# Means of the first two tiles by products over columns of the transposed input, later loads of the row-major input, and a re-ordered start, product stage and tail

## The chip, the cores and the metric

The kernel runs on one core of a Trainium2 chip. The metric is the device time of one execution in microseconds (us). Three executions of the kernel before took 243.49, 243.72 and 243.82 us, so the median is 243.72 us. The execution that was profiled took 243.56 us.

The core has five engines with instruction streams of their own: TensorE (PE in the profile; its weight loads are listed as PEld), VectorE (DVE), ScalarE (ACT), GpSimd (POOL) and SyncE (SP, which here only issues transfers). They wait for each other through semaphores. Transfers issued by SP, ACT and POOL share the core's 16 DMA engines.

## The reference, cut to what matters

The input x has 8 x 256 rows of 512 numbers, which the kernel sees as 16 tiles of 128 rows.

```python
xn = _layernorm(x, axis=-1)                         # (x - m) / sqrt(v + 1e-5)
q = (xn @ Wq.T + bq)                                # 32 heads of 128
q_sel = (elu(q) + 1)[:, :, ::4, :]                  # every fourth head: 8 heads, 1024 columns
num = einsum('bshd,hde->bshe', q_sel, M)
den = einsum('bshd,hd->bsh', q_sel, z)[..., None] + 1e-6
out_heads = repeat(num / den, 4, axis=2)
out = x + out_heads.reshape(b, s, 4096) @ Wo.T + (xn @ (w_int8 * w_scale) + b)
```

The keys and values do not reach the output. Since each retrieved head is repeated four times, the four matching blocks of Wo can be added first. Since M comes before Wo, each head needs one matrix P_g = M_g times that summed block (128 x 512).

## The kernel before, in words

**Precision.** Each of the large products is made of three passes in the format fp32r: the operands are split into a high part (`_hi`, a copy rounded by ACT) and a low part (`_lo`, the rest, subtracted by DVE), and PE computes hi times hi, hi times lo and lo times hi. Each pass is one instruction with 128 rows of weights and 512 columns.

**Stages.** For each tile t:

- the mean and the variance of the rows come from the row-major tile x (`moments`: one BN_STATS, one BN_AGGR, and the variance plus epsilon), and GpSimd makes the reciprocal root (`rstd_of`);
- the mean is spread over all partitions by a PE transpose (`spread_mean`) and subtracted from the transposed tile xT. For tiles 0 to 2 DVE does it straight from the accumulator bank (`center_first`, `center`); from tile 3 on ACT copies the mean (`copy_mean`) and POOL subtracts it (`center`);
- ACT makes `xT_hi` and DVE `xT_lo`; PE makes q in two halves (`product_q(t, 0)` and `(t, 1)`, 12 instructions each) and the dense part (`product_dense(t)`, 12 instructions into the one bank `dense_ps`, which DVE has to empty by `add_dense(t - 1)` first);
- DVE scales and biases q (`add_bias`), ACT takes the exponential (`exp_of`), DVE forms s = elu + 1 (`make_s`); POOL multiplies by z (`times_z`), DVE sums and inverts (`denominator`), ACT scales (`make_a`), DVE transposes 32 x 32 blocks (`turn_blocks`), and 16 small transfers move the blocks to where they belong (`spread_blocks`, issued by SP, at the end also by ACT and POOL as `spread_group` and `spread_last_group`). ACT and DVE split the result (`copy_aT_hi`, `split_aT_lo`), and PE makes `product_attn(t)` of 24 instructions. DVE adds it to x, and SP stores the tile.

**Start.** Wq (2 MB) comes in eight pieces or fewer, and PE works on tiles 0 and 1 together, in an order written out by hand, as the pieces arrive. Before that, PE runs products of zeros (`keep_busy`).

**Wo.** The four blocks of Wo arrive in two halves j: the first block by a plain load (`load_wo(j)`), three more by POOL transfers that add while they write (`add_wo(r, j)`, 1 MB each). Each of these waits until the one before it on the same half has landed, and everything behind it on POOL waits with it. When all three have landed on half 0, PE may make P_0 to P_3 (`product_P`, one plain fp32 product of 512 columns each); half 1 gives P_4 to P_7. The banks `attn_ps` alternate, so P_g for g >= 2 waits until DVE has split P_(g-2) (`split_P_lo`).

**Order.** There is no scheduler. Each engine's order is the order of the calls in its block (`@block.sync`, `gpsimd`, `scalar`, `vector`, `tensor`), written out by hand up to tile 6 and by a loop from tile 7 (`LEAD`) on. Within one engine nothing overtakes.

The whole of it is below, with the line numbers that the profile uses.

Of the kernel before, what the change touches and what calls it, by code (L numbers as in the profile page):

```python
# [18 lines left out]
def retrieval_and_dense(nc, x_d, xT_d, WqT_d, bq_d, WoT_d, MT_d, z_d, w_d, wscale_d, b_d, out_d):  # L19
# [19 lines left out]
    with ExitStack() as ctx:  # L39
# [28 lines left out]
        ident = sb("ident", [P, P])  # L68
        e_and_sz = sb("e_and_sz", [P, E + G * (D + 1)])
# [34 lines left out]
        wq_half_in = [sem(f"wq_half_in{i}") for i in range(4)]  # L104
        wq_in = [sem(f"wq_in{k}") for k in range(2, K)]
# [5 lines left out]
        consts_set = sem("consts_set")  # L111
        eps_set = sem("eps_set")
# [77 lines left out]
        def _(sp):  # L190
# [11 lines left out]
            def load_wq(k):  # L202
                sp.dma_start(WqT_raw[:, k, :], WqT_d[0, k]).then_inc(wq_in[k - 2], 16)

# [38 lines left out]
            load_wo(1)  # L243
            sp.dma_start(MT[:], MT_d).then_inc(M_in, 16)
            load_x(4)
            load_xT(4)
            sp.dma_start(z_b[:], z_d.unsqueeze(0).to_broadcast([P, E])).then_inc(z_in, 16)
            sp.dma_start(b_b[:], b_d.unsqueeze(0).to_broadcast([P, HID])).then_inc(b_in, 16)
            for t in range(5, FIRST_LENT):
                load_x(t)  # L250
                load_xT(t)
# [27 lines left out]
        def _(pool):  # L279
            def rstd_of(t):  # L280
                pool.wait_ge(vareps_ready, t + 1)
# [10 lines left out]
            def scale_w():  # L292
                pool.wait_ge(wscale_in, 16)
                pool.wait_ge(w_cast, 2)
                nc.gpsimd.tensor_tensor(wd_raw[:, K // 2:, :], w_f32[:, K // 2:, :], wd_raw[:, K // 2:, :], ALU.mult
# [27 lines left out]
            def spread_last_group(t):  # L323
                pool.wait_ge(a_turned, t + 1)
                pool.wait_ge(aT_lo_ready, 2 * t - 2)
                for j in range(4):
                    nc.gpsimd.dma_start(aT_place(t)[j * 32:(j + 1) * 32, 3, :],
                                        sbuf_s[96:128, t % SRING, j * E // 4:(j + 1) * E // 4]).then_inc(aT_in_by_pool[t - FIRST_SHARED - 1], 16)

            nc.gpsimd.memset(neg_half[:], -0.5).then_inc(consts_set, 1)  # L330
# [8 lines left out]
            pool.wait_ge(wd_by_pool, 1)  # L339
# [4 lines left out]
            add_wo(1, 1)  # L344
            rstd_of(4)
# [200 lines left out]
        def _(dve):  # L546
            def statistics(t):
                dve.wait_ge(x_in[t], 16)
                if t >= 2:
                    dve.wait_ge(meanvar_ready, t - 1)  # L550
# [455 lines left out]
```

## Time and profile before

| what | value |
|---|---|
| median of three executions | 243.72 us |
| profiled execution | 243.56 us |
| its span, first to last instruction | 241.7 us |
| PE busy | 234.1 us, 97% of the span |
| DVE busy | 178.0 us, 74% |
| ACT busy | 119.6 us, 49% |
| POOL busy | 108.4 us, 45% |
| moved by transfers | 34.83 MB |

Read it with three things in mind. The span leaves out 1.9 us of the execution that lie around it. PE's busy time counts overlapping records and the products of zeros at the start, so a busy PE says that it had an instruction in flight, not that it was at its peak. And a share is an average over the start, the stage in which Wo is added, the steady loop and the tail, which have different limits.

### The profile page before, as it was taken

To read this page: it belongs to the slowest core of one execution; us is meant where nothing else is said; L and a number is where in the kernel's file an instruction comes from. 1 tells how busy PE (TensorE), PEld (TensorE's weight loads), DVE (VectorE), ACT (ScalarE), POOL (GpSimd) and SP (SyncE) were. 2 spreads that over 40 slices of the span, in tenths; PEclk is the share of its full clock that TensorE was granted. 3 is DMA by queue.
4 is the path that set the end of the run, shared out by engine and by line. 5 is a ranking of instruction groups with operands and counts; after the bars stand their busy time and mean duration, and the time that the engine had idled before them with its cause. 6 is when DMAs were issued, how large, how long until landed. Compare 5 with 4: busy or idle time off the path is not lost.

```text
span 241.7 us, 3385 instructions
## 1 busy us (share of the span) xinstructions
PE 234.1 (97%) x1030; PEld 186.7 (77%) x1030; DVE 178.0 (74%) x266; ACT 119.6 (49%) x276; POOL 108.4 (45%) x108
## 2 busy tenths in 40 slices
PE   8699999998999999999999999999999999999995
PEld 2488788885776788888888888888888888788885
DVE  2889695897998669887687694958666778995631
ACT  2654626628648923655463526455463747341110
POOL 1058734756271815553434326263403629657500
PEclk9999999999999999999999999999999999999999
DMA  7999999999370211424252515221212223244441
GB/s 225 405 417 411 383 242 225 216 217 217 94 252 5 53 51 52 127 54 126 53 168 53 161 50 169 52 91 42 88 52 73 56 75 108 76 136 136 133 174 44
DMA packets 21985, 34.83 MB, mean 144 GB/s; under 512 B 5200, under 2 KB 13136, under 8 KB 20816
## 3 DMA queue, kind: packets, MB, share of 16 engines
q1 hardware_dynamic: 19344, 26.63, 33.4%
q0 software_dynamic: 1376, 6.82, 13.4%
q10 hardware_dynamic: 1248, 1.18, 1.8%
q8 instruction: 8, 0.13, 0.2%
q14 instruction: 9, 0.07, 0.1%
HBM read 22.02 MB, written 4.19 MB: 108 GB/s over the span
## 4 chain that ended last, share of the span: by engine, by line
PE 33%; issue 31%; POOL 18%; DVE 8%; SPq 4%; DMA 2%; ACT 2%; ACTq 1%; POOLq 0%; DVEq 0%
POOL e_and_sz L313 9%; POOL xT L288 5%; PE attn_ps L793 4%; PE attn_ps L794 4%; PE attn_ps L795 4%; SPq L219 4%; POOL x L321 3%; PE q_ps L793 3%; PE q_ps L795 3%; PE q_ps L794 3%; DVE aT_lo L654 2%; PE dense_ps L793 2%; PE dense_ps L795 2%; PE dense_ps L794 2%; DMA xT<-in_xT 2%
## 5 line engine op out<-in xcount | busy, mean ns | idle before, releaser
L313 POOL TENSOR_TENSOR e_and_sz<-s,z_b 128x512 f32<-128x512 f32 x32 | 42.0, 1340 | 40.3 <-DVE den L633 40.2
L441 ACT ACTIVATE s<-s,rden 128x128 f32<-128x128 f32 x128 | 39.2, 389 | 40.5 <-DVE rden L637 40.5
L793 PE MATMUL attn_ps<-P_hi,aT_hi 128*128 128x512 f32 (+1 forms) x128 | 49.8, 389 | 0.5 <-DVE aT_lo L654 0.5
L795 PE MATMUL attn_ps<-P_hi,aT_lo 128*128 128x512 f32 (+1 forms) x128 | 49.1, 383 | 0.0
L794 PE MATMUL attn_ps<-P_lo,aT_hi 128*128 128x512 f32 (+1 forms) x128 | 49.0, 383 | 0.0
L793 PE MATMUL q_ps<-WqT_hi,xT_hi 128*128 128x512 f32 x104 | 42.1, 405 | 0.3 <-DVE s L628 0.3
L795 PE MATMUL q_ps<-WqT_hi,xT_lo 128*128 128x512 f32 x104 | 40.6, 390 | 0.0
L794 PE MATMUL q_ps<-WqT_lo,xT_hi 128*128 128x512 f32 x104 | 40.5, 389 | 0.0
L288 POOL TENSOR_TENSOR xT<-xT,mean_b 128x512 f32<-128x512 f32 x13 | 18.3, 1408 | 37.8 <-ACT mean_b L390 31.2
L621 DVE SCALAR_TENSOR_TENSOR q_ps<-q_ps,rstd,bq_b 128x512 f32<-128x512 f32 x28 | 21.0, 753 | 19.3 <-PE q_ps L795 19.3
L793 PEld LDWEIGHTS attn_ps<-P_hi,aT_hi 128*128 128x128 f32 x128 | 24.1, 188 | 6.2 <-issue 0.9
L795 PEld LDWEIGHTS attn_ps<-P_hi,aT_lo 128*128 128x128 f32 x128 | 24.1, 188 | 4.9
L794 PEld LDWEIGHTS attn_ps<-P_lo,aT_hi 128*128 128x128 f32 x128 | 24.1, 188 | 4.4
L793 PE MATMUL dense_ps<-wd_hi,xT_hi 128*128 128x512 f32 x64 | 25.9, 405 | 0.0
L795 PE MATMUL dense_ps<-wd_hi,xT_lo 128*128 128x512 f32 x64 | 25.0, 390 | 0.0
L794 PE MATMUL dense_ps<-wd_lo,xT_hi 128*128 128x512 f32 x64 | 24.9, 390 | 0.0
L793 PEld LDWEIGHTS q_ps<-WqT_hi,xT_hi 128*128 128x128 f32 x104 | 19.5, 188 | 5.7 <-issue 1.7
L628 DVE SCALAR_TENSOR_TENSOR s<-q_ps,e_and_sz 128x512 f32<-128x512 f32 x28 | 18.7, 677 | 6.9 <-ACT e_and_sz L430 3.2
L794 PEld LDWEIGHTS q_ps<-WqT_lo,xT_hi 128*128 128x128 f32 x104 | 19.5, 188 | 4.6 <-issue 0.7
L633 DVE TENSOR_REDUCE den<-e_and_sz 128x8 f32<-128x1032 f32 x16 | 19.4, 1214 | 4.8 <-POOL e_and_sz L313 4.8
L428 ACT ACTIVATE e_and_sz<-q_ps 128x512 f32<-128x512 f32 x28 | 16.6, 591 | 12.5 <-DVE q_ps L621 12.5
L795 PEld LDWEIGHTS q_ps<-WqT_hi,xT_lo 128*128 128x128 f32 x104 | 19.5, 188 | 4.2
(82 smaller groups left out, 365.3 us busy)
## 6 DMA issues: line engine op xcount, KB each, us to landing
x<-in_WoT POOLq DMA_DIRECT2D x6, 1024.0 KB, 10.6
x<-in_x SPq DMA_DIRECT2D x16, 256.0 KB, 3.9
xT<-in_xT SPq DMA_DIRECT2D x16, 256.0 KB, 4.1
aT<-s SPq DMA_DIRECT2D x124, 32.0 KB, 1.9
out<-x SPq DMA_DIRECT2D x15, 256.0 KB, 2.3
MT<-s SPq DMA_DIRECT2D x96, 32.0 KB, 1.9
x<-in_WoT SPq DMA_DIRECT2D x2, 1024.0 KB, 14.0
s<-in_WqT SPq DMA_DIRECT2D x2, 512.0 KB, 7.1
```

What stands on the lines that cost most here:

```text
L219: sp.dma_start(aT_place(t)[j * 32:(j + 1) * 32, i, :], sbuf_s[i * 32:(i + 1) * 32, t % SRING, j * E // 4:(j + 1) * E // 4]).then_inc(aT_in ...
L288: nc.gpsimd.tensor_tensor(xT[:, t % XRING, :, :], xT[:, t % XRING, :, :], mean_b[:, t % 2, :].unsqueeze(1).to_broadcast([P, K, P]), ALU.su ...
L313: nc.gpsimd.tensor_tensor(sz_eps[:, :, h * D // 2:(h + 1) * D // 2].rearrange("p g (j c) -> p j g c", j=2), by_quarter(sbuf_s[:, t % SRING ...
L321: nc.gpsimd.tensor_tensor(x[:, t, :], x[:, t, :], b_b[:], ALU.add).then_inc(b_added, 1)
L428: nc.scalar.activation(e, q_bank(t, h)[:], ACT.Relu, scale=-1.0).then_inc(qneg_ready, 1)
L441: last = nc.scalar.activation(a_g, a_g, ACT.Copy, scale=rden[:, t % 2, g:g + 1])
L621: nc.vector.scalar_tensor_tensor(q_bank(t, h)[:], q_bank(t, h)[:], rstd[:, t:t + 1], bq_b[:, halves(h)], ALU.mult, ALU.add).then_inc(q_bia ...
L628: nc.vector.scalar_tensor_tensor(sbuf_s[:, t % SRING, halves(h)], q_bank(t, h)[:], 0.0, ebuf[:, halves(h)], ALU.max, ALU.add).then_inc(s_r ...
L633: nc.vector.reduce_sum(den[:, t % 2, :], sz_eps, AX.X).then_inc(den_ready, 1)
L793: nc.tensor.matmul(out, x_hi, w_hi, start=start, stop=False)
L794: nc.tensor.matmul(out, x_hi, w_lo, start=False, stop=False)
L795: return nc.tensor.matmul(out, x_lo, w_hi, start=False, stop=stop)
```

## The change

1. **Means of tiles 0 and 1.** They no longer come from x. For tile 0 PE multiplies a matrix of 1/512 with the four column chunks of xT (four plain fp32 products of 128 columns, added in `mean_ps`). For tile 1 DVE first adds the four chunks (`sum_chunks_of_second`, a reduction over a strided view of 512 elements into 128), and PE makes one such product into the bank `q_ps[2]`. The moments of tiles 0 and 1, of which now only the variance and the product's scale are needed, move back behind those of tile 2 and of tile 3.
2. **Loads.** SP starts with xT of tile 0 and seven halves of Wq; ACT issues the first half of Wq and xT of tile 1. x of tiles 0 and 1 follow behind xT of tile 2. Further down, tiles 4, 5 and 6 come ahead of z, M and b, and M (512 KB) and b (256 KB) stand between tile 6 and tile 7.
3. **POOL** scales the first half of w (DVE the second), computes the root of tile 1 later, and centres tile 6 ahead of the last `add_wo`, with both halves of `times_z(1)` ahead of the one before it.
4. **DVE, ACT and PE** are re-ordered up to tile 7, and PE makes the dense part of tile 5 and the first half of q of tile 6 ahead of P_0.
5. **Tail.** ACT makes `aT_hi` of tile 11 ahead of the four transfers of `spread_group(12)`.

SP's loads, first before, from `load_wo(0)` on (Wo x2, M, tile 4, z, b, tiles 5, 6 and 7; `x` and `xT` are a tile's two forms, `MT`, `z_b` and `b_b` are M, z and b):

```order
L206 DMA x<-in_WoT 128x2048 x2
L244 DMA MT<-in_MT 128x1024
L192 DMA x<-in_x 128x512
L197 DMA xT<-in_xT 128x512
L247 DMA z_b<-in_z 128x1024
L248 DMA b_b<-in_b 128x512
L192 DMA x<-in_x 128x512
L197 DMA xT<-in_xT 128x512
L192 DMA x<-in_x 128x512
L197 DMA xT<-in_xT 128x512
```

The same stretch of SP now, from `load_wo(0)` to x of tile 7:

```order
L212 DMA x<-in_WoT 128x2048
L201 DMA x<-in_x 128x512
L206 DMA xT<-in_xT 128x512
L212 DMA x<-in_WoT 128x2048
L201 DMA x<-in_x 128x512
L206 DMA xT<-in_xT 128x512
L256 DMA z_b<-in_z 128x1024
L201 DMA x<-in_x 128x512
L206 DMA xT<-in_xT 128x512
L259 DMA MT<-in_MT 128x1024
L260 DMA b_b<-in_b 128x512
L201 DMA x<-in_x 128x512
```

Tile 7 stood directly behind tile 6; now M and b stand between them, and z behind tile 5.

PE before, from the end of `product_q(5, 1)` (bank q3) over P_0 to the start of `product_q(6, 0)` (bank q0):

```order
L794 MATMUL q3_ps<-WqT_lo,xT_hi 128x512
L795 MATMUL q3_ps<-WqT_hi,xT_lo 128x512
L856 MATMUL attn0_ps<-x,MT 128x512
L793 MATMUL q0_ps<-WqT_hi,xT_hi 128x512
L794 MATMUL q0_ps<-WqT_lo,xT_hi 128x512
```

PE now, at the end of `product_q(5, 1)`, where the mean of tile 7 and the dense part of tile 5 follow:

```order
L800 MATMUL q3_ps<-WqT_hi,xT_lo 128x512
L808 MATMUL mean_ps<-ident,meanvar 128x128
L798 MATMUL dense_ps<-wd_hi,xT_hi 128x512
L799 MATMUL dense_ps<-wd_lo,xT_hi 128x512
L800 MATMUL dense_ps<-wd_hi,xT_lo 128x512
```

and 24 instructions on, where `product_q(6, 0)` ends and P_0 and P_1 stand side by side:

```order
L799 MATMUL q0_ps<-WqT_lo,xT_hi 128x512
L800 MATMUL q0_ps<-WqT_hi,xT_lo 128x512
L872 MATMUL attn0_ps<-x,MT 128x512
L872 MATMUL attn1_ps<-x,MT 128x512
L798 MATMUL q1_ps<-WqT_hi,xT_hi 128x512
```

P_0 moved behind 25 instructions, and the dense part of tile 5, which came after P_1, now comes before both.

ACT's tail before, around `spread_group(12)` (the four transfers into MT) and `copy_aT_hi(11)` (the rows behind them):

```order
L452 ACTIVATE aT_hi<-MT 128x512 x2
L441 ACTIVATE s<-s,rden 128x4x32 x8
L459 DMA MT<-s 32x256 x4
L452 ACTIVATE aT_hi<-aT 128x512 x2
L441 ACTIVATE s<-s,rden 128x4x32 x8
```

and now:

```order
L465 ACTIVATE aT_hi<-MT 128x512 x2
L454 ACTIVATE s<-s,rden 128x4x32 x8
L465 ACTIVATE aT_hi<-aT 128x512 x2
L472 DMA MT<-s 32x256 x4
L454 ACTIVATE s<-s,rden 128x4x32 x8
```

The copy for tile 11 changed places with the transfers for tile 12.

The diff, cut to its core:

```diff
+        def mean_in(t):
+            return (q_ps[2] if t == 1 else mean_ps)[:, 0:P]
+
+        def moments_before(t):
+            return [1, 3, 0, 2][t] if t <= 3 else t
...
-            load_x(0)
             load_xT(0)
+            load_wq_half(0, 1)
             load_wq_half(1, 0)
-            load_x(1)
             load_wq_half(1, 1)
-            load_xT(1)
-            load_wq(2)
+            load_wq_half(2, 0)
+            load_wq_half(2, 1)
+            load_wq_half(3, 0)
+            load_wq_half(3, 1)
             load_x(2)
             load_xT(2)
-            load_wq(3)
+            load_x(0)
+            load_x(1)
...
+            scale_w()
             rstd_of(0)
-            rstd_of(1)
             rstd_of(2)
-            scale_w()
...
             times_z(1, 0)
+            times_z(1, 1)
             add_wo(3, 0)
-            times_z(1, 1)
+            center(6)
             add_wo(3, 1)
-            center(6)
...
+            def sum_chunks_of_second():
+                dve.wait_ge(xT_in[1], 16)
+                nc.vector.reduce_sum(x_sum[:], xT[:, 1, :, :].rearrange("p k r -> p r k"), AX.X).then_inc(x_sum_ready, 1)
...
-            statistics(0)
-            mean_and_variance(0)
             center_first(0)
+            center_first(1)
+            split_first_xT_lo(0)
             split_wq_lo(0, 0)
-            split_first_xT_lo(0)
-            center_first(1)
+            sum_chunks_of_second()
+            split_first_xT_lo(1)
             split_wq_lo(0, 1)
-            statistics(1)
-            mean_and_variance(1)
             center(1)
...
+            def mean_of_columns(t):
+                if t == 0:
+                    pe.wait_ge(mean_weights_set, 1)
+                    pe.wait_ge(xT_in[0], 16)
+                    for k in range(K):
+                        last = nc.tensor.matmul(mean_in(0), mean_weights[:], xT[:, 0, k, :], start=k == 0, stop=k == K - 1)
+                else:
+                    pe.wait_ge(x_sum_ready, 1)
+                    last = nc.tensor.matmul(mean_in(1), mean_weights[:], x_sum[:], start=True, stop=True)
+                last.then_inc(mean_filled, 1)
...
-            keep_busy(8)
-            pe.wait_ge(consts_set, 3)
-            spread_mean(0)
-            keep_busy(6)
+            keep_busy(4)
+            mean_of_columns(0)
+            keep_busy(3)
             hi_hi(0, 0, 0)
-            hi_lo(0, 0, 0)
...
```

Unchanged, and used by the prediction, is DVE's order from `add_dense(3)` on: `moments(7)`, `add_bias(4, 1)`, `denominator(1)`, `turn_blocks(0)`, `make_s(4, 0)`, `split_xT_lo(6)`, `make_s(4, 1)`, `add_bias(5, 0)`, `add_dense(4)`.

## Rows read from the trace of the kernel before

**Rows 1.** The page: busy time, share of the span, instructions.

```profile
PE 234.1 (97%) x1030; PEld 186.7 (77%) x1030; DVE 178.0 (74%) x266; ACT 119.6 (49%) x276; POOL 108.4 (45%) x108
```

**Rows 2.** Stretches: length, busy us per engine, granted clock, DMA share, GB/s.

```profile
6.80:20.21 13.41, 12.16 (x51) 9.06 (x51) 12.12 (x25) 7.87 (x13) 4.53 (x4) 1.00 1.04 414
20.21:56.74 36.53, 36.21 (x161) 29.30 (x159) 28.78 (x48) 18.54 (x39) 22.83 (x22) 1.00 1.04 269
84.45:210.64 126.19, 126.19 (x560) 103.85 (x558) 95.36 (x136) 62.88 (x157) 55.82 (x49) 1.00 0.29 85
```

**Rows 3.** PE's waits: who it waited for, us, times, longest.

```profile
PE attn_ps L856 <- issue: 1.0, 1, 1.0
PE attn_ps L815 <- ACT xT_hi L405: 1.0, 1, 1.0
PE attn_ps L793 <- DVE aT_lo L654: 0.5, 1, 0.5
PE q_ps L793 <- DVE s L628: 0.3, 1, 0.3
```

**Rows 4.** Timeline of the start: start, us, engine, line [idle before <-releaser].

```profile
3.20 0.69 DVE L551 BATCH_NORM_STATS2 stats<-x 128x6 f32<-128x512 f32 x1 [2.27 <-DMA x<-in_x]
...
5.26 0.42 DVE L569 TENSOR_TENSOR xT<-xT,mean_ps 128x256 f32<-128x256 f32 x1 [1.15 <-DMA xT<-in_xT]
...
9.88 0.69 DVE L576 TENSOR_TENSOR xT<-xT,mean_ps 128x512 f32<-128x512 f32 x1 [0.41 <-PE mean_ps L803]
...
11.29 0.50 PE L815 MATMUL attn_ps<-WqT_hi,xT_hi 128*128 128x512 f32 x1 [0.96 <-ACT xT_hi L405]
...
20.21 0.39 PE L793 MATMUL q_ps<-WqT_hi,xT_hi 128*128 128x512 f32 x1
```

**Rows 5.** Issue and landing of xT of tile 6, and of x of tile 7.

```profile
L197 SPq DMA_DIRECT2D xT<-in_xT x1: 2982/2982/2982, 18.4 to 18.4; - x1
...
DMA to landing us min/median/max: 25.0/25.0/25.0
...
L192 SPq DMA_DIRECT2D x<-in_x x1: 759/759/759, 21.4 to 21.4; - x1
...
DMA to landing us min/median/max: 27.6/27.6/27.6
```

**Rows 6.** POOL's adding transfers of Wo: timeline, and the page's median to landing.

```profile
25.25 1.98 POOL L303 DMA_DIRECT2D x<-in_WoT  x2
...
47.62 0.90 POOL L303 DMA_DIRECT2D x<-in_WoT  x1 [1.55 <-DMA x<-in_WoT]
...
x<-in_WoT POOLq DMA_DIRECT2D x6, 1024.0 KB, 10.6
```

**Rows 7.** DVE from moments(7) to add_dense(4), and POOL's centring of tile 6.

```profile
49.09 0.69 DVE L551 BATCH_NORM_STATS2 stats<-x 128x6 f32<-128x512 f32 x1
...
55.71 2.34 DVE L589 TENSOR_TENSOR xT_lo<-xT,xT_hi 128x512 fp32r<-128x512 f32 x1 [1.81 <-ACT xT_hi L405]
...
59.23 0.73 DVE L641 SCALAR_TENSOR_TENSOR x<-dense_ps,rstd,x 128x512 f32<-128x512 f32 x1
...
53.42 1.59 POOL L288 TENSOR_TENSOR xT<-xT,mean_b 128x512 f32<-128x512 f32 x1
```

**Rows 8.** PE at the first product P (two records to one product).

```profile
56.51 0.39 PE L795 MATMUL q_ps<-WqT_hi,xT_lo 128*128 128x512 f32 x1
57.88 1.10 PE L856 MATMUL attn_ps<-x,MT 128*128 128x512 f32 x2 [0.98 <-issue]
```

**Rows 9.** DVE's sum over 1032 elements, from the page.

```profile
L633 DVE TENSOR_REDUCE den<-e_and_sz 128x8 f32<-128x1032 f32 x16 | 19.4, 1214 | 4.8 <-POOL e_and_sz L313 4.8
```

**Rows 10.** ACT and DVE in the tail.

```profile
206.70 2.70 ACTq L459 DMA_DIRECT2D MT<-s  x4
209.50 1.15 ACT L452 ACTIVATE aT_hi<-aT 128x512 fp32r<-128x512 f32 x2 [5.03 <-issue]
...
210.16 1.62 DVE L654 TENSOR_TENSOR aT_lo<-aT,aT_hi 128x512 fp32r<-128x512 f32 x2 [0.48 <-ACT aT_hi L452]
```

More of the change, by code:

```diff
@@ L103, in retrieval_and_dense @@
         xT_in = [sem(f"xT_in{t}") for t in range(T)]
-        wq_half_in = [sem(f"wq_half_in{i}") for i in range(4)]
-        wq_in = [sem(f"wq_in{k}") for k in range(2, K)]
+        wq_half_in = [sem(f"wq_half_in{i}") for i in range(2 * K)]
         wo_in = [sem(f"wo_in{j}") for j in range(J)]
@@ L389, in copy_mean @@
                     act.wait_ge(xc_by_pool, t - 4)
-                nc.scalar.activation(mean_b[:, t % 2, :], mean_ps[:, 0:P], ACT.Copy
+                nc.scalar.activation(mean_b[:, t % 2, :], mean_in(t), ACT.Copy
                                      ).then_inc(mean_copied, 1)
@@ L683, in _ @@
             split_wq_lo(3, 0)
+            split_wq_lo(3, 1)
+            moments(0)
             center(2)
-            split_wq_lo(3, 1)
             split_xT_lo(2)
@@ L688, in _ @@
             moments(3)
+            split_wd_lo(0)
             add_bias(0, 0)
+            split_wd_lo(1)
             add_bias(0, 1)
-            split_wd_lo(0)
-            split_wd_lo(1)
+            make_s(0, 0)
             split_xT_lo(3)
+            moments(1)
+            moments(4)
+            add_dense(0)
             add_bias(1, 0)
-            moments(4)
-            make_s(0, 0)
             make_s(0, 1)
@@ L699, in _ @@
             add_bias(2, 0)
-            add_dense(0)
             moments(5)
@@ L703, in _ @@
             make_s(1, 0)
+            add_dense(1)
             add_bias(3, 0)
@@ L706, in _ @@
             split_xT_lo(4)
-            add_dense(1)
             make_s(2, 0)
@@ L729, in _ @@
             make_s(5, 0)
+            turn_blocks(1)
+            make_s(5, 1)
+            denominator(2)
+            add_dense(5)
+            add_bias(6, 0)
             split_P_lo(0)
-            make_s(5, 1)
-            add_bias(6, 0)
             split_P_lo(1)
-            turn_blocks(1)
-            add_dense(5)
-            denominator(2)
+            make_s(6, 0)
+            split_xT_lo(7)
+            add_bias(6, 1)
+            moments(8)
             split_P_lo(2)
-            make_s(6, 0)
-            add_bias(6, 1)
-            split_xT_lo(7)
+            denominator(3)
+            make_s(6, 1)
             split_P_lo(3)
-            moments(8)
-            denominator(3)
             add_dense(6)
-            make_s(6, 1)
+            split_aT_lo(0)
             split_P_lo(4)
-            split_aT_lo(0)
             turn_blocks(2)
+            split_P_lo(5)
             for t in range(LEAD, T):
                 add_bias(t, 0)
-                if t == LEAD:
-                    split_P_lo(5)
                 if t + 2 < T:
@@ L905, in _ @@
                 hi_lo(1, h, 1)
-                lo_hi(1, h, 1)
-            hi_lo(0, 0, 2)
             hi_hi(0, 1, 2)
             lo_hi(0, 1, 2)
-            hi_lo(0, 1, 2)
-            spread_mean(2)
+            for h in range(2):
+                lo_hi(1, h, 0)
+                lo_hi(1, h, 1)
             for h in range(2):
@@ L914, in _ @@
                 lo_hi(1, h, 2)
-                hi_lo(1, h, 2)
+            pe.wait_ge(consts_set, 3)
+            spread_mean(2)
             for t in range(2):
                 for h in range(2):
-                    hi_hi(t, h, 3)
-                    lo_hi(t, h, 3)
-                    hi_lo(t, h, 3).then_inc(q_filled, 1)
+                    hi_lo(t, h, 2)
+            for h in range(2):
+                hi_hi(0, h, 3)
+                lo_hi(0, h, 3)
+                hi_lo(0, h, 3).then_inc(q_filled, 1)
+            for h in range(2):
+                hi_hi(1, h, 3)
+                lo_hi(1, h, 3)
+                hi_lo(1, h, 3).then_inc(q_filled, 1)
             product_q(2, 0)
```

141 lines of the change are left out of this document (69 added, 72 removed).

## The prediction, made before the changed kernel ran

> **What bounds the kernel now.** I read the shares first. PE is busy for 97% of the span and the next engine for 74% [rows 1], so PE is the bound, and the question is how many of its microseconds are not work. The stretches come second [rows 2]. In the steady stretch from 84.45 to 210.64 PE started 560 instructions in 126.19 us, one each 0.225 us, with no idle time. Nothing can be won there, only shifted. The table of PE's waits shows all that is left [rows 3]: 1.0 us at a product P, 1.0 us at the start for the high part of tile 1, 0.5 us in the tail, 0.3 us at a q. A record of PE lasts about 0.39 us while the next starts after 0.23, so an idle time understates a wait by 0.16 us. At P_0 the starts are 56.51 and 57.88, 1.37 us apart in place of 0.23, so that wait costs 1.14 us [rows 8]. The tail's costs 0.5 + 0.16, about 0.65 us.
>
> Before its first real product at 6.80 PE has nothing to do: DVE begins to centre tile 0 at 5.26, on the landing of xT, and centres tile 1 at 9.88 after its moments; PE then starts tile 1 at 11.29 and tile 2 at 20.21 [rows 2, 4]. From 6.80 to 20.21 DVE is busy for 12.12 of 13.41 us and the transfers are at 1.04 of capacity with 414 GB/s, that is 0.63 us for 256 KB [rows 2]. The start is bound by DVE and the order of loads, not by PE.
>
> From 20.21 to 56.74 the DMA share is still 1.00 and above, at 269 GB/s: here Wo is added. The clock column is 1.00 in all stretches, so the clock is no term of the sum.
>
> **Part 1: the start.** Removed from DVE ahead of tile 1 are two statistics. Added is one reduction of 512 elements. DVE's 1032 elements take 1.21 us [rows 9], so 512 take about 0.65 if the stride costs nothing and 1.3 if it costs as much again. I take 0.65; the first is the nearer row in kind, but it has no such stride. PE's fp32 product of 512 columns shows two records in 1.10 us less an overlap of about 0.25 [rows 8], so 0.86, and one of 128 columns is a quarter, 0.21. Four make 0.86 us, or 1.7 if PE then ran at the lower of its two levels. xT of tile 0 now is the first transfer; the first one landed at about 3.2, where DVE began its statistics [rows 4]. So the centring can begin between 4.3 and 5.2 against 5.26; I take 4.9.
>
> From there I walked DVE: two halves centred 0.75, split 0.35, first Wq low part 0.65, the sum 0.65, second half split 0.35, Wq low part 0.65. Each is a DVE instruction of 0.69 us for 512 elements [rows 4], which starts 0.65 after the last. That ends near 8.4, and tile 1 is centred until about 9.2 against 10.57 before. PE has tile 1's high part near 9.9 and then 36 instructions left of the 48, without a wait: 9.9 + 36 x 0.23 + 0.2 = 18.4 for tile 2. The gain is 1.8 us at this point, with bounds of 0 and 2.4. Moving the moments of tiles 0 and 1 back adds 2.1 us to DVE behind 20 us, where it was idle for 36.53 - 28.78 = 7.75 us up to 56.74 [rows 2]; so I cost it at nothing. If that idle time were not where it is needed, PE would wait up to 2 us at the dense part of tile 0 or q of tile 3, and the start would be given back. The 0.3 us at the q of tile 3 goes too, since DVE now forms the first s before that tile. PE should be about 2.3 us early at 30.
>
> **Part 2: P_0.** It is moved behind 25 instructions (5.5 us). It waits for the third addition on half 0, issued at 47.62 and landing 10.6 us (median) later, near 58 [rows 6]. PE reaches it no earlier than 60, so the wait of 1.14 us goes. The additions hold the DMA engines in series, 5.3 us each, and their total is unchanged.
>
> What is late next stands in the moved rows. The dense part of tile 5 is now made before P_0 and q of tile 6, and needs `dense_ps` empty, so it waits for `add_dense(4)`. DVE did that at 59.23 to 59.96 [rows 7], where before it was needed only after P_1. Its chain from `moments(7)` at 49.09 [rows 7] is 4.8 us of work up to the first s of tile 4, then a wait of 1.81 us for tile 6's high part, and a split of 2.34 us where 0.68 is normal. Both waits come from POOL, which centred tile 6 at 53.42 only, behind the last addition. With `center(6)` ahead of it they go: 4.8 + 4 x 0.65 = 7.4 us from `moments(7)` to an empty bank. PE would be ready for the dense part at 56.74 + 0.1 - 2.3 = 54.5.
>
> **Part 3: when can DVE begin `moments(7)`?** Two conditions. First, its own chain: it hangs on `center(5)`, behind the landing of the second addition, whose first issue at 25.25 [rows 6] moves to about 23.5 as POOL centres tile 3 earlier; so 1.8 us earlier, 47.3. Second, x of tile 7 must be there. Before, it landed at 21.4 + 27.6 = 49.0, just as DVE came to it [rows 5, 7]. xT of tile 6 landed at 18.4 + 25.0 = 43.4. So while Wo is added, one load of 256 KB lands each 5.6 us, not each 0.63: the load takes turns with the additions.
>
> The Trainium skill states this ("DMA: Bandwidth & Descriptors", section "Queues, rings and completion order"): each DMA engine goes round the queues that have work, packet by packet. By that rule each load that stands behind the first addition costs a whole addition, whatever its own size, and the trace agrees with 5.6 us.
>
> The change puts M (512 KB) and b in front of tile 7 and moves the additions up by about 1.8 us. Against that, x and xT of tiles 5 and 6 and z go ahead. Before, x and xT of tile 6 and x of tile 7 landed in such turns: 49.0 - 3 x 5.6 = 32.2, some 6 us after the additions' first issue, and all that stood ahead of tile 6 had come at full rate. In the same way I now let all up to x of tile 6 come at full rate, till about 30, and count M, b and x of tile 7 as three whole turns behind a rest of tile 6's xT (M's a little longer): 31.0 + 6.2 + 5.6 + 5.6 = 48.4. It is 47 if the rest is gone, and each turn more adds 5.6.
>
> So the bank is empty at 48.4 + 7.4 + 0.1 = 55.9, and PE begins the dense part there rather than at 54.5. Before, without P_0, it would have stood there at 56.85. The gain at this point is 0.95 us: much of the start's gain is lost here.
>
> **Part 4: the rest.** In the product stage PE needs s, the low parts of P and tile 8, all of which follow turn_blocks(0), which moves with DVE by 0.7 us or more; by my walk each is there 0.2 to 1 us ahead. In the tail, ACT's copy for tile 11 waited until 209.50 behind four transfers issued at 206.70 [rows 10]. That wait is put down to issue, not to a transfer, so its input was there; I put it near 205.5. DVE then is the next to be late: it is free at 210.16 - 0.48 = 209.68 [rows 10] and gives the first half at 210.3, before PE's 210.64 (the steady stretch's pace up to there). The 0.65 us goes, and the four transfers start no later than before, since what released them at 206.70 is not ACT's copy.
>
> **Sum.** 0.95 + 1.14 + 0.65 = 2.75 us. From the profiled execution's 243.56 this is 240.8. That execution lies 0.16 below the median of 243.72, inside the spread of the three, so I say 240.9.
>
> **Rivals.**
> - *Tile 7 is early enough.* If x of tile 7 lands before 47.3, the dense part starts at 54.8. The gain is 2.05 + 1.14 + 0.65 = 3.85 us, so 239.8. For it: the median DMA engine is turns ahead of the last one. Against: the wait is for the last one.
> - *Tile 7 comes a turn later (slower).* At 54.0 the dense part starts at 61.5, 4.65 us later than before, and 243.56 + 4.65 - 1.79 = 246.4. It decides as soon as x of tile 7 lands after 51.2. For it: the loads stand behind two more, and the additions start sooner. Against: the loads ahead drain at 0.63 us until the additions move data, which before was some 4 us after their issue. The skill's rule above is this rival's rule; it gives 246.4 if one load more than I count is left behind the first addition.
> - *The start gives nothing* (a costly strided sum, slow fp32 products). Then POOL's issue stays at 25.25, DVE reaches `moments(7)` at 49.1, and the dense part starts at 56.5. The gain is 0.35 + 1.14 + 0.65, so 241.4.
> - *The moved waits cancel.* With tile 7 at 50.5 to 51.2 the time is 243 to 243.6.
>
> **Numbers.** About 0.2% (0.5 us) is what a measurement of this kernel can tell from no change. The forecast (240 to 242) has 0.42, the early tile 7 0.20, the start without gain 0.12, the cancelling case 0.07 (two thirds of it within 0.2%), the late tile 7 0.19. So faster 0.76, same 0.05, slower 0.19. The likeliest case's own range is 239.9 to 242.2; the range for 8 in 10 is 239.4 to 244.4.
>
> **What would show it.** PE's first product of tile 2 near 18.4 (part 1). No wait at the products P, and one at the dense part of tile 5 with DVE's `add_dense` as releaser, starting near 56 (parts 2 and 3). x of tile 7 landing at 47 to 49.5, and DVE waiting for it at its statistics for about 1 us. ACT's copy for tile 11 before 207 and no PE wait near 208 (part 4). I am wrong if DVE waits at those statistics beyond 51, or if PE waits among P_2 to P_7.

## The result: 1.2% slower, and the profile after

The changed kernel takes 246.92 us (median of four executions, 245.78 to 251.86), where the kernel before took 243.69 in the same comparison. The ratio is 1.0118 with a 95% interval of 1.0069 to 1.0166; the ratios leave out an execution that lies over 1.5% above the fastest of its kernel, here the one of 251.86 us. I had said 240.9, with 244.4 as the upper end. The profiled execution took 247.59 us, with a span of 245.8.

PE's waits after, in the view that answers to [rows 3] (who it waited for, us, times, longest):

```profile
PE dense_ps L798 <- DVE x L650: 3.8, 1, 3.8
PE dense_ps L891 <- DVE warm L672: 1.0, 1, 1.0
PE mean_ps L815 <- DMA xT<-in_xT: 1.0, 1, 1.0
PE attn_ps L798 <- DVE aT_lo L663: 0.5, 1, 0.5
```

The waits for P_0, for tile 1's high part and for s are gone, as forecast. The tail's is still there, and there is one of 3.8 us at the dense part of tile 5, which waits for `add_dense(4)`. I had forecast that wait, but of 1.4 us. Its surroundings in the timeline (start, us; DVE and POOL answer to [rows 7]):

```profile
42.56 1.61 POOL L300 TENSOR_TENSOR xT<-xT,mean_b 128x512 f32<-128x512 f32 x1
...
44.36 2.81 POOL L325 TENSOR_TENSOR e_and_sz<-s,z_b 128x512 f32<-128x512 f32 x2
...
44.86 2.87 DVE L598 TENSOR_TENSOR xT_lo<-xT,xT_hi 128x512 fp32r<-128x512 f32 x1 [1.31 <-ACT xT_hi L418]
...
49.51 0.74 DVE L650 SCALAR_TENSOR_TENSOR x<-dense_ps,rstd,x 128x512 f32<-128x512 f32 x1
52.17 0.69 DVE L565 BATCH_NORM_STATS2 stats<-x 128x6 f32<-128x512 f32 x1 [1.93 <-DMA x<-in_x]
...
55.16 2.52 POOL L325 TENSOR_TENSOR e_and_sz<-s,z_b 128x512 f32<-128x512 f32 x2 [1.10 <-DVE den L642]
...
56.91 1.32 DVE L598 TENSOR_TENSOR xT_lo<-xT,xT_hi 128x512 fp32r<-128x512 f32 x1
...
59.41 0.73 DVE L650 SCALAR_TENSOR_TENSOR x<-dense_ps,rstd,x 128x512 f32<-128x512 f32 x1
```

```profile
56.14 0.27 PE L808 MATMUL mean_ps<-ident,meanvar 128*128 128x128 f32 x1
60.20 0.50 PE L798 MATMUL dense_ps<-wd_hi,xT_hi 128*128 128x512 f32 x1 [3.79 <-DVE x L650]
```

DVE waits for x of tile 7 until 52.17 at its statistics, beyond the 51 that I had named as the sign of being wrong. But the next cause is in the same rows: DVE finished `add_dense(3)` at 50.2 only, where I had it ready at 47.3, and two low-part splits take 2.87 and 1.32 us where 0.68 is normal. Each ends about 0.55 us after the POOL operations beside it (`times_z`, the rows with `e_and_sz`).

The landing of x of tile 7, as in [rows 5] (issue, then time to landing):

```profile
L201 SPq DMA_DIRECT2D x<-in_x x1: 433/433/433, 20.9 to 20.9; - x1
...
DMA to landing us min/median/max: 31.2/31.2/31.2
```

Last, PE's granted clock, in stretches (start:end, length, PE busy, clock, DMA share, GB/s):

```profile
56.00:60.00 4.00, 0.41 (x3) 1.00 1.02 212
60.00:62.00 2.00, 1.80 (x6) 0.80 0.83 197
62.00:64.00 2.00, 2.00 (x6) 0.50 0.30 82
64.00:66.00 2.00, 2.00 (x9) 0.85 0.20 51
```

After the 3.8 us without work the clock fell to half (from 2.4 to 1.2 GHz), and eight products started 0.43 us apart in place of 0.23. That is 1.6 us that my sum did not have.

The account at PE: the dense part of tile 5 starts at 60.20, 3.35 us later than the 56.85 at which PE would have reached it before without P_0; P_0's 1.14 us are saved; the clock costs 1.6; the end is 0.2 later. That is +4.0, against 245.8 - 241.7 = 4.1 us of span. The clock alone does not make the loss: the one execution whose mean clock was 1.00 took 245.78 us, still 2.1 us more than before.

### The profile page after: what moved, and what is told of

Its sections match the earlier page's. It is cut to its first block, busy times and chain, and to the rows that moved or that the text cites. A ratio compares the mean times of both kernels' runs of the same rounds, so it can differ in the third digit from the quotient of the medians.

```text
span 245.8 us, 3390 instructions
## 1 busy us (share of the span) xinstructions
PE 236.8 (96%) x1031; PEld 189.9 (77%) x1031; DVE 182.7 (74%) x267; ACT 120.2 (49%) x276; POOL 108.0 (44%) x109
## 4 chain that ended last, share of the span: by engine, by line
issue 30%; PE 29%; POOL 17%; DVE 8%; SPq 8%; DMA 3%; ACT 2%; POOLq 0%; DVEq 0%; ACTq 0%
POOL e_and_sz L325 8%; SPq L225 7%; POOL xT L300 4%; POOL x L333 4%; PE q_ps L800 3%; PE q_ps L798 3%; PE q_ps L799 3%; DVE aT_lo L663 3%; PE dense_ps L798 3%; PE dense_ps L800 2%; PE dense_ps L799 2%; DMA aT<-s 2%; PE attn_ps L798 2%; PE attn_ps L800 2%; PE attn_ps L799 2%
## 5 line engine op out<-in xcount | busy, mean ns | idle before, releaser
L325 POOL TENSOR_TENSOR e_and_sz<-s,z_b 128x512 f32<-128x512 f32 x32 | 41.8, 1336 | 38.9 <-DVE den L642 38.8
L800 PE MATMUL attn_ps<-P_hi,aT_lo 128*128 128x512 f32 (+1 forms) x128 | 49.1, 383 | 0.0
L798 PE MATMUL q_ps<-WqT_hi,xT_hi 128*128 128x512 f32 x104 | 41.6, 400 | 0.0
L798 PE MATMUL dense_ps<-wd_hi,xT_hi 128*128 128x512 f32 x64 | 26.7, 418 | 3.8 <-DVE x L650 3.8
L800 PE MATMUL dense_ps<-wd_hi,xT_lo 128*128 128x512 f32 x64 | 25.6, 401 | 0.0
L799 PE MATMUL dense_ps<-wd_lo,xT_hi 128*128 128x512 f32 x64 | 25.6, 400 | 0.0
```

What stands on the lines that cost most here:

```text
L325: nc.gpsimd.tensor_tensor(sz_eps[:, :, h * D // 2:(h + 1) * D // 2].rearrange("p g (j c) -> p j g c", j=2), by_quarter(sbuf_s[:, t % SRING ...
L798: nc.tensor.matmul(out, x_hi, w_hi, start=start, stop=False)
L799: nc.tensor.matmul(out, x_hi, w_lo, start=False, stop=False)
L800: return nc.tensor.matmul(out, x_lo, w_hi, start=False, stop=stop)
```

## Experiments

Each kernel is the changed one with the edit shown, if no other base is named. Ratios are against the kernel before (243.6 to 243.7 us).

### x7_ahead: x of tile 7 in front of M and b

```diff
             load_xT(6)
+            load_x(7)
             sp.dma_start(MT[:], MT_d)...
```

> The changed kernel with one load moved: x of tile 7 directly behind tile 6's loads, ahead of M and b. Theory A (x of tile 7 is one turn of 5.6 us too late): it lands near 40 to 41 in place of 52.15, DVE begins the statistics of tile 7 at 50.2 where it was free, the dense part of tile 5 starts at 58.2 in place of 60.2, PE waits 1.9 us there instead of 3.8, and the granted clock stays near 1.00: 246.2 - 2.0 - 0.9 to 1.6 = 242.6 to 243.3 us. Rival B (the additions of Wo are the bound, whatever DVE does): the dense part still starts after 59.5 and the time stays within 0.5 us of 246.2.

245.77 us, ratio 1.008 [1.0052, 1.0108].

```profile
49.45 0.68 DVE L564 BATCH_NORM_STATS2 stats<-x 128x6 f32<-128x512 f32 x1
...
54.17 2.48 DVE L597 TENSOR_TENSOR xT_lo<-xT,xT_hi 128x512 fp32r<-128x512 f32 x1
...
57.83 0.73 DVE L649 SCALAR_TENSOR_TENSOR x<-dense_ps,rstd,x 128x512 f32<-128x512 f32 x1
...
58.62 0.50 PE L797 MATMUL dense_ps<-wd_hi,xT_hi 128*128 128x512 f32 x1 [2.59 <-DVE x L649]
```

x of tile 7 lands at 41.9, DVE no longer waits for it, and the dense part starts 1.6 us earlier. So A has that step, but not the size of the gain: by its time alone the run would pass for B, and its interval overlaps with that of the changed kernel. The rest of the wait is DVE's: the split of tile 6 now takes 2.48 us, since it falls beside POOL's two `times_z`. The clock fell all the same. Its ten executions price that: the four with a mean clock of 1.00 took 244.26 to 244.66 us, the five with 0.992 or 0.993 took 245.73 to 246.80, and the one with 0.986 took 247.47. The clock costs about 1.4 us where it falls once. (In the profiled execution the clock was 0.53 from 60 to 62 and 0.62 from 62 to 64. That is 1.7 us lost, or a mean of 0.993 over 244 us, so 0.986 looks like two falls. Where it fell in the executions without a profile is not shown.)

### moments7_behind: the statistics of tile 7 after the bank is emptied

```diff
             add_dense(3)
-            moments(7)
             add_bias(4, 1)
...
             add_dense(4)
+            moments(7)
```

(and `spread_mean(7)` behind `product_dense(5)` on PE)

> The changed kernel with the moments of tile 7 behind add_dense(4) on DVE, and the mean of tile 7 behind the dense part of tile 5 on PE; the loads stay as they are, so x of tile 7 still lands near 52. Theory A (only the order on DVE makes that landing matter): DVE goes on at 50.2 with 6.4 us of work up to the empty bank, the dense part of tile 5 starts at 56.7, PE waits about 0.6 us there, no fall of the clock: 246.2 - 3.5 - 1.6 = 241.1 us. Rival B (PE is held further on by the additions or by tile 7's centring): the 3.5 us come back as a wait at P_0, at q of tile 7 or among P_4 to P_7, and the time stays above 244.

245.97 us, ratio 1.010 [1.0083, 1.0117].

```profile
53.39 2.83 POOL L325 TENSOR_TENSOR e_and_sz<-s,z_b 128x512 f32<-128x512 f32 x2
...
53.49 3.28 DVE L598 TENSOR_TENSOR xT_lo<-xT,xT_hi 128x512 fp32r<-128x512 f32 x1
...
58.75 0.50 PE L798 MATMUL dense_ps<-wd_hi,xT_hi 128*128 128x512 f32 x1 [2.71 <-DVE x L650]
```

The time is B's (above 244), but its mechanism is not: the dense part starts 2 us later than A said, and none of B's later waits appears. The split of tile 6 lasts as long as the two POOL operations beside it and then its own 0.6 us. The late load and the stretched split cover each other: take one away, and most of the other appears.

### fill_wait: PE kept busy during the wait

```diff
             spread_mean(7)
+            fill_wait(16)      # 16 products of zeros into q_bank(6, 0)
             product_dense(5)
```

> The changed kernel with 16 products of zeros (bf16, 128x512) between the mean of tile 7 and the dense part of tile 5, into a bank that the next product overwrites. The wait itself stays: the dense part still starts at 60.1 to 60.2. Theory A (the idle PE loses its clock): the granted clock stays at 1.00 over the stretch from 60 to 66, the eight products that took 0.43 us each take 0.23, and the time falls by about 1.6 us to 244.6. Rival B (the clock fell for another reason, such as an event outside the kernel): the same eight products are slow again in this profile, and the time stays at 246.2 +- 0.5.

Four executions took 245.18, 245.30, 248.95 and 252.68 us. The ratio on record, 1.0147 [1.0058, 1.0235], is not that of the two lower ones (1.007) and decides nothing; the profile, of the first of them, says more. The dense part started at 59.35, not at 60.1 (x of tile 7 landed 0.9 us earlier here), and the clock held:

```profile
60.00:62.00 2.00, 2.00 (x10) 1.00 0.84 207
62.00:64.00 2.00, 2.00 (x10) 1.00 0.28 74
```

In the profiles theory A holds: the clock fell behind the unfilled wait and not behind the filled one. The single executions are weaker evidence. The executions of 245.18 and 245.30 us have a mean clock of 1.00, but those of 248.95 and 252.68 have 0.993, so their clock fell somewhere even so, and one of the changed kernel's four had 1.00 without the filling.

### P0_first: PE's old order

```diff
             product_q(5, 1)
+            product_P(0)
+            product_q(6, 0)
+            product_P(1)
             spread_mean(7)
             product_dense(5)
```

(and P_2, q, P_3 behind it, as before)

> The changed kernel with PE's old order from P_0 to the dense part of tile 6: P_0, first half of q of tile 6, P_1, mean of tile 7, dense part of tile 5, P_2, second half of q of tile 6, P_3. Theory A (the new order put DVE's late bank in front of PE): PE waits at P_0 for the third addition until 58.4 (2.2 us) and no more at the dense part, which it reaches at 62 with the bank empty since 60.1; everything behind is 1.6 us earlier: 244.6 us, or 243.0 if the clock stays at 1.00 as well. Rival B (the additions land later because they were issued differently): P_0 starts after 59.5 and the time is 246 or more.

247.96 us, ratio 1.018 [1.0165, 1.0195]. A missed the time by 3.4 us; it lies where B had it, but B's late P_0 is not there.

```profile
57.96 1.10 PE L872 MATMUL attn_ps<-x,MT 128*128 128x512 f32 x2 [1.73 <-issue]
...
67.73 1.19 PE L872 MATMUL attn_ps<-x,MT 128*128 128x512 f32 x1 [2.19 <-DVE P_lo L621]
```

P_0 started when A said, so the additions are not late. But I had left DVE in its new order, with `add_dense(5)` ahead of `split_P_lo(0)`, and P_2 waited for that. It was an ill-made test of the old order: PE's and DVE's orders belong together.

The same profile holds something else. x of tile 7 landed at 48.0 here, where the prediction had it, with the same order of loads as in the changed kernel:

```profile
50.15 0.68 DVE L565 BATCH_NORM_STATS2 stats<-x 128x6 f32<-128x512 f32 x1
...
58.36 0.74 DVE L650 SCALAR_TENSOR_TENSOR x<-dense_ps,rstd,x 128x512 f32<-128x512 f32 x1
```

DVE still came to its statistics at 50.15 only, and had the bank empty at 59.1, against 55.8 forecast and 60.1 in the changed kernel. So most of the lateness is DVE's own chain, and not the landing.

### center5_ahead: DVE's chain freed of POOL

```diff
 (loads as in x7_ahead; POOL:)
+            center(5)
             add_wo(2, 1)
-            center(5)
 (DVE:)
+            split_xT_lo(5)
             denominator(0)
-            split_xT_lo(5)
```

> The changed kernel with x of tile 7 ahead of M and b (as in x7_ahead), POOL's centring of tile 5 ahead of add_wo(2, 1) in place of behind it, and on DVE the low part of tile 5 ahead of the denominator of tile 0, so that no POOL operation runs beside it. Theory C (DVE's chain to the empty bank is late since it starts behind an addition's landing and since splits beside a POOL operation take 2.3 to 3.3 us in place of 0.68): tile 5 is centred near 38.5 in place of 42.6, the split takes 0.7, DVE begins the statistics of tile 7 near 47, the bank is empty near 55, PE waits less than 0.5 us at the dense part of tile 5 (starting 56 to 56.3), the clock stays at 1.00: 241.3 to 242.2 us. Rival D (the wait moves to P_0, as the additions land at 58 and 63.5 in any case): PE waits 1 us or more at P_0 or at P_4, and the time is 243 or more. Rival E (centring ahead of the issue delays the additions): the second half's landings move from 63 to 65 and the time is above 243.

The profiled execution took 241.35 us, with no wait of PE between 10 and 200 us. But the ten executions spread up to 245.32, with a median of 243.94: ratio 0.9989 [0.996, 1.0018], no difference from before. The profiled execution is C's; the median lies above 243, where D and E had it, though their waits are not in the profile. C names what can be reached, and does not yet explain the spread.

### center5_warm6: six products of zeros at the start

```diff
-            keep_busy(4)
+            keep_busy(6)
             mean_of_columns(0)
```

> As center5_ahead, and six products of zeros in place of four ahead of the mean of tile 0, which close PE's idle 0.7 to 1.0 us before the landing of xT. Theory F (the idle time kept PE at the lower level until 9.5): the products from 6.9 on start every 0.23 us in place of 0.43, PE then waits for the high part of tile 1 until 11.0 to 11.2, tile 2 begins near 19.4 in place of 19.8, and the time is 0.3 to 0.5 us less than that of center5_ahead. Rival G (PE needs its real products to rise): the starts stay 0.43 us apart until 9.5, and the time is the same within 0.2.

243.54 us, ratio 0.9999 [0.9979, 1.0019]. Its profile shows what I take to vary between the executions of center5_ahead (of those only one has a profile):

```profile
36.33 1.58 POOL L324 TENSOR_TENSOR e_and_sz<-s,z_b 128x512 f32<-128x512 f32 x1
37.59 1.57 POOL L299 TENSOR_TENSOR xT<-xT,mean_b 128x512 f32<-128x512 f32 x1
...
36.44 3.28 DVE L597 TENSOR_TENSOR xT_lo<-xT,xT_hi 128x512 fp32r<-128x512 f32 x1
```

In center5_ahead's own profile the same split began at 35.87, ahead of these two, and took 0.68:

```profile
35.87 0.68 DVE L597 TENSOR_TENSOR xT_lo<-xT,xT_hi 128x512 fp32r<-128x512 f32 x1
...
37.06 1.60 POOL L324 TENSOR_TENSOR e_and_sz<-s,z_b 128x512 f32<-128x512 f32 x1
```

POOL runs the two as soon as an addition has landed. Here POOL got there 0.7 us earlier and DVE 0.6 us later than in center5_ahead, and that costs DVE 2.6 us; PE waits 0.71 us for that split, until 39.77. For the start, F is not shown: PE's products ran at full pace from 6.4 on and tile 2 began at 19.24, but in center5_ahead's profile, with four products of zeros, they ran at full pace from 7.2 on and tile 2 began at 19.36.

### before_act_tail and before_pool_tail: part 4 alone

Both are the kernel before. The first moves ACT's copy alone:

```diff
-            spread_group(FIRST_SHARED + 1)
             copy_aT_hi(FIRST_SHARED)
+            spread_group(FIRST_SHARED + 1)
```

> The kernel before with ACT's copy for tile 11 ahead of the four transfers of tile 12 and nothing else (part 4 of the change alone). Theory H (DVE is stretched by POOL's addition of b): ACT is ready 1 us or more earlier, but DVE's split of tile 11 starts at 209.7 beside a POOL operation of 1.3 us and takes 2.0 to 2.2 us for its two halves, PE still waits about 0.5 us there, and the time stays within 0.2 of before (243.6). The prediction's step: the wait goes and the time falls by 0.65 us to 243.0.

The second has POOL add b to tiles 9 to 11 earlier as well:

```diff
                 for u in denominators_of_step(t):
+                    if u == T - 2:
+                        for v in range(3):
+                            add_b(T - LEAD + v)
                     times_z(u, 0)
```

> As before_act_tail, and POOL adds b to tiles 9, 10 and 11 in its idle time of 6.6 us up to 198, ahead of times_z(14), in place of behind 200, 204 and 209. Theory H: DVE's split of tile 10 takes 1.2 to 2 us in place of 3.02 and that of tile 11 takes 1.3 us, starting near 208.5; PE does not wait at 211, and the time falls by 0.65 us to 243.0. Rival I (the stretched splits have another cause, such as the operand in MT): they take 3.0 and 1.6 to 2.2 us as before and the wait of 0.5 us stays: 243.6.

The first: 243.75 us, ratio 1.0004 [0.9994, 1.0013]; the second: 242.98, ratio 0.9969 [0.9956, 0.9983]. The first one's tail (its second row is the split for tile 11):

```profile
203.84 3.03 DVE L654 TENSOR_TENSOR aT_lo<-MT,aT_hi 128x512 fp32r<-128x512 f32 x2
...
209.85 2.18 DVE L654 TENSOR_TENSOR aT_lo<-aT,aT_hi 128x512 fp32r<-128x512 f32 x2
...
209.56 1.30 POOL L321 TENSOR_TENSOR x<-x,b_b 128x512 f32<-128x512 f32 x1
```

The second one's:

```profile
203.81 1.93 DVE L658 TENSOR_TENSOR aT_lo<-MT,aT_hi 128x512 fp32r<-128x512 f32 x2
...
208.73 1.28 DVE L658 TENSOR_TENSOR aT_lo<-aT,aT_hi 128x512 fp32r<-128x512 f32 x2
```

Theory H holds on both sides. The 0.65 us of part 4 were real, but ACT's move alone does not give them: with POOL's additions out of the way as well, both splits shorten, and PE's wait is gone. POOL's edit without ACT's was not run. Both are probably needed: before, DVE's split for tile 11 waited for ACT's copy of 209.50 [rows 10], and here it begins at 208.73.

### start_alone: the new start with the old middle and tail

From the first load of Wo on, the loads are those of before; the engines' orders are the new ones up to tile 4, and those of before from there on.

> Only the changed start (means of tiles 0 and 1, the first loads, and the orders up to tile 4); from the first load of Wo on, the loads, POOL, ACT, DVE and PE follow the kernel before, and so does the tail. Theory J (the start gains 0.5 us at tile 2, and nothing of it passes P_0, which waits for the third addition at 57.9): tile 2 begins at 19.2 to 19.8, P_0 starts at 57.7 to 58.2 after a wait of 1.5 us or more, and the time is 243.2 to 243.9, that is the same as before. The prediction's view (2 us early at 30, usable behind): 241.5 to 242.5. Rival K (the start does harm by itself): above 244.5.

248.26 us, ratio 1.0171 [1.014, 1.0202]. K was right: the start does harm by itself. The profiled execution took 246.25 us, the least of the four, so it shows 2.5 of the 4.5 us:

```profile
19.68 0.50 PE L795 MATMUL q_ps<-WqT_hi,xT_hi 128*128 128x512 f32 x1 [0.42 <-DVE xT_lo L594]
...
45.15 0.50 PE L795 MATMUL dense_ps<-wd_hi,xT_hi 128*128 128x512 f32 x1 [2.91 <-DVE x L646]
```

```profile
42.08 0.69 DVE L561 BATCH_NORM_STATS2 stats<-x 128x6 f32<-128x512 f32 x1 [2.67 <-DMA x<-in_x]
...
53.31 0.69 DVE L561 BATCH_NORM_STATS2 stats<-x 128x6 f32<-128x512 f32 x1 [2.65 <-DMA x<-in_x]
```

x of tiles 6 and 7 land near 42.1 and 53.3, the latter 4.2 us later than the 49.1 of before [rows 5]. The same bytes are asked for in the same order behind Wo, but POOL issues the additions earlier (24.52 against 25.25 [rows 6]). My reading, which the next two runs test, is that more loads are then left to take turns with them.

### start_alone_hold and after_hold: the first addition held back

```diff
             center(3)
+            pool.wait_ge(x_in[6], 16)
             add_wo(1, 0)
```

> start_alone, with POOL waiting for x of tile 6 before it issues the first addition of Wo. In start_alone x of tile 6 landed at 42.06 and x of tile 7 at 53.28, where the kernel before had 37.84 and 49.06, and DVE waited 2.67 and 2.65 us for them. Theory N (each load that an engine still has when the additions move data takes a turn of 5.6 us, so what counts is how many loads are left then): x of tile 6 now lands near 30.5 and x of tile 7 before 37, DVE's two waits and PE's 2.9 us at the dense part of tile 3 are gone; the additions end 2 to 5 us later (third landings at 60 to 63 and 66 to 69), so that P_0 now waits for them: 244 to 247 us. Rival O (the late landings have another cause, such as the loads themselves or the queue): x of tile 6 still lands after 36.

> The changed kernel as it is, with POOL waiting for x of tile 6 before it issues the first addition of Wo (24.46 before, about 30 now). Theory N: xT of tile 6, M, b and x of tile 7 then are behind no addition or one, x of tile 7 lands before 40 in place of 52.15 and DVE does not wait at its statistics; the additions end 2 to 5 us later and the wait of PE is at the products P. 243 to 246 us. Rival O: x of tile 7 lands after 45 still, and DVE waits for it.

248.1 us, ratio 1.0167 [1.0127, 1.0207], and 246.23 us, ratio 1.0112 [1.0075, 1.0148]. In after_hold (issue of x of tile 7, time to landing, and POOL's first and last issues of additions):

```profile
L201 SPq DMA_DIRECT2D x<-in_x x1: 432/432/432, 20.3 to 20.3; - x1
...
DMA to landing us min/median/max: 12.5/12.5/12.5
```

```profile
29.88 1.99 POOL L315 DMA_DIRECT2D x<-in_WoT  x2 [5.99 <-DMA x<-in_x]
...
54.06 0.88 POOL L315 DMA_DIRECT2D x<-in_WoT  x1 [1.55 <-DMA x<-in_WoT]
```

x of tile 7 lands at 32.8 in place of 52.1, and in start_alone_hold DVE's two waits are gone as well. N is right on the landings of the loads. Both times lie above its ranges. In start_alone_hold the additions, held back by 7.4 us, end 3.9 us later, as N had it, and PE waits 0.68 us at P_0. In after_hold, held back by 5.4 us, they end only 0.6 to 0.8 us later (58.96 and 64.30 against 58.37 and 63.53), where N had 2 to 5. The time is not better, since the roots and the centring of tile 4 stand behind the held issue on POOL: PE now waits 0.79 and 1.04 us between 32 and 39 (2.63 and 1.05 us, up to 41, in start_alone_hold).

### all_mended and all_mended_warm6: the changed kernel, mended

center5_ahead, with the POOL edit of before_pool_tail and on DVE:

```diff
             add_dense(1)
+            split_xT_lo(4)
             add_bias(3, 0)
             make_s(1, 1)
-            split_xT_lo(4)
```

> The changed kernel with x of tile 7 ahead of M and b, tile 5 centred ahead of add_wo(2, 1), its low part ahead of the denominator of tile 0, the low part of tile 4 two instructions earlier on DVE (ahead of the POOL operations that follow an addition's landing), and b added to tiles 9, 10 and 11 in POOL's idle time up to 202. Theory C (DVE's lateness by stretched splits is the cause of the loss, and of the spread of center5_ahead from 241.4 to 245.3): no PE wait over 0.3 us between 20 and 200, none in the tail, 240.6 to 241.2 us, and a spread below 1 us. Rival L (the spread comes from loads that land a turn later in some executions): the median stays above 242.5 with a spread of 3 us or more. Rival D (a wait takes its place at P_0 or P_4): above 243.

> As all_mended, with six products of zeros in place of four ahead of the mean of tile 0. Theory F (the start's products run at the full level from 6.4 on): tile 2 begins 0.3 to 0.5 us earlier than in all_mended, and if nothing behind takes it back the time is 240.2 to 240.9. Rival M (the gain at tile 2 is lost in a wait for a low part or an empty bank between 20 and 56): the time is that of all_mended within 0.2, or more.

241.14 us (240.91 to 242.47), ratio 0.9908 [0.9888, 0.9928], and 241.13 us, ratio 0.9903 [0.9885, 0.9921]. Theory C holds, with a spread of 1.6 us in place of 4 (it had said below 1); M is right on the second. The split of tile 6 is back at its normal length, and these are all of PE's waits in all_mended that the view lists:

```profile
51.18 0.67 DVE L601 TENSOR_TENSOR xT_lo<-xT,xT_hi 128x512 fp32r<-128x512 f32 x1
```

```profile
PE dense_ps L894 <- DVE warm L675: 1.0, 1, 1.0
PE mean_ps L818 <- DMA xT<-in_xT: 0.5, 1, 0.5
PE q_ps L821 <- DVE x_sum L576: 0.4, 1, 0.4
PE q_ps L801 <- DVE xT_lo L601: 0.3, 1, 0.3
PE attn_ps L875 <- DVE P_lo L624: 0.2, 1, 0.2
PE q_ps L834 <- ACT xT_hi L411: 0.2, 1, 0.2
```

It is 2.6 us faster than the kernel before. PE begins the dense part of tile 5 at 55.6 against 56.85 (1.25 us), P_0 does not wait (1.14), the tail does not (0.65); some 0.4 us are lost among the products P. The forecast of 240.9 is thus within reach, but for a kernel with five things mended that the prediction took as they were. Of these only the load's move (x7_ahead) and, on the kernel before and with ACT's move, POOL's additions of b were run without the others.

## Why the prediction was wrong, step by step

- **Part 1, the start (1.8 us at tile 2): mis-sized.** The high part of tile 1 came at 11.2, not at 9.9. xT landed at 3.7 and the centring began at 5.95 (I took 4.9), and the strided sum took 1.07 us (I took 0.65, inside my bounds). PE in turn reached tile 1 only at 11.64: after the idle time ahead of the mean its starts stayed 0.43 us apart until 9.5. Tile 2 began at 19.76, 0.45 us earlier than before. This start varies between executions: in after_hold's profile, where xT landed earlier, tile 2 began at 18.99.
- **Part 2, P_0 (1.14 us): right.** Without a wait, P_0 began at 67.36, though it was far behind by then. That the dense part of tile 5 would wait for `add_dense(4)` was right too. The chain of 7.4 us from the statistics to the empty bank was 8.0, and 9.1 in x7_ahead, because the splits were stretched.
- **Part 3, the time at which DVE empties the bank (55.8, measured 60.1): the step that failed.** It hangs on two conditions, and both came late. *First, x of tile 7 (48.4).* The turns were right (6.2 us for M, then 5.6 each): M landed at 40.9, b at 46.6, x at 52.1. The starting point was wrong: xT of tile 6 still took a turn and landed at 34.8, where I had let it come by 31. The rival "a turn later" is what happened (dense part at 60.2, forecast 61.5), and I gave it 0.19. That its time of 246.4 is close is partly luck: the dense part started 1.3 us earlier than it says, and the clock, which it does not have, cost 1.6. The two hold runs show what decides: how many loads are left when the additions begin to move data. In start_alone an issue 0.73 us earlier went with landings 4.2 us later, so a forecast to the microsecond was not to be had here, and my range should have said so. I also counted turns as if the transfer moved as one. The trace holds sixteen landing steps for each transfer, and the last counts: in the changed kernel fifteen steps of x of tile 7 had come by 47.3 and the last came at 52.2, and before the change 41.1 and 49.1.
- **Part 3, *second*, DVE's own chain (47.3, measured 50.2): the larger share.** With x of tile 7 out of the way the dense part still started at 58.6 (x7_ahead), 2.7 of the 4.3 us behind the forecast, and the median was still 2 us above the kernel before. I let the second addition land 1.8 us earlier since the first would be issued earlier. The first was issued at 24.46 and not at 23.5, and the issue does not set the landings: the first addition landed at 35.6 against 36.2, the second at 41.7 against 41.8, and tile 5 was centred at 42.56 against 42.70. Then its split took 2.87 us.
- **Part 4, the tail (0.65 us): size right, cause wrong.** ACT was early, as forecast, but DVE was late by a stretched split, so PE's wait of 0.5 us stayed.
- **No term at all: the clock (1.6 us).** I read 1.00 in every stretch of before and carried it over, to a kernel for which I forecast a longer wait.

## What stretches DVE

The splits of xT and aT subtract one SBUF tile from another, and take 0.68 us alone (two halves of aT 1.28). Beside POOL's element-wise operations they took 1.3 to 3.3 us; DVE's operations with an accumulator bank as one input kept their 0.65 to 0.75. The Trainium skill has this as a rule ("SBUF — State Buffer", section "Who interferes with whom"): a DVE instruction with two SBUF inputs contends with a GpSimd instruction that reads SBUF, and the one that comes second is blocked until the first is done. The runs agree, and add one thing: beside two POOL operations in a row (2.83 us together) the split took 3.28 us, so it waited for both. The sign was in [rows 7] before the change: 2.34 us for such a split. I had put it down to POOL's late centring, which would move away, and misread the rows: that centring ended at 55.01, and the split began at 55.71. What ran beside it was `times_z`, a row that [rows 7] does not have:

```profile
54.67 2.82 POOL L313 TENSOR_TENSOR e_and_sz<-s,z_b 128x512 f32<-128x512 f32 x2
```

The split ended at 58.05, some 0.56 us behind it. So taking the centring away could not by itself give the 1.7 us that I took off DVE's chain for it; in the changed kernel this split took 1.32 us, again beside `times_z`.

## What to carry to other kernels

When a step of DVE with two SBUF inputs takes longer than its like, look for the POOL operation beside it, and place such steps where POOL waits. When loads share the DMA engines with large transfers, count how many are left as those begin to move data, give each a whole turn, and put the first one needed in front: an earlier issue of the large transfers can make the loads later and nothing earlier. And once a sum has a PE wait of a few microseconds in it, price the clock as a case of its own.

## What I had not expected of the hardware

- In x7_ahead's profile the clock fell to 1.2 GHz 1.5 us after PE had begun work again behind an idle time of 2.59 us, and six of its ten executions have a mean clock below 1.00; a fall cost 1.4 us. The idle time alone does not decide: in start_alone_hold PE was idle for 2.63 us and the granted clock was 1.00 in every stretch from 30 to 44.
- Nor does the clock column show all: it says 1.00 from 8 to 10 us in the changed kernel, where products started 0.43 us apart.
- In after_hold, additions held back by 5.4 us landed less than 1 us later (in start_alone_hold 7.4 us cost 3.9). From the first issue to the last landing they took 34.4 us in after_hold and 39.1 in the changed kernel. So a load that takes turns with them pays a whole turn in its own landing, but costs them little more than when it goes ahead.
- With the same order of loads and of POOL's work, the landing of x of tile 7 moved between profiles (48.0 in P0_first, 49.7 in moments7_behind, 51.3 in fill_wait, 52.1 in the changed kernel). In P0_first POOL issued the first addition at 25.06, 0.6 to 1.0 us later than in the others, but among those others a later issue goes with a later landing. What moves it, and whether it makes the slowest executions of the changed kernel (251.86 us), stays open: only profiled executions show landings.
